# A routed low-rank residual layer: one subtraction per tile moved from GpSimd to VectorE, and another moved forward in VectorE's order

## The chip, the cores and the metric

The kernel runs on one core of one Trainium2 chip. The time is the device time of one execution in microseconds, and of several executions the median is taken. Beside it stands one profiled execution, whose trace is read here. Five engines work side by side, each with its own in-order queue: TensorE (PE in the profile; its weight loads are listed apart as PEld and overlap the matmuls), VectorE (DVE), ScalarE (ACT), GpSimd (POOL) and SyncE (SP), which here only issues transfers. They meet through semaphores.

## The reference

For each of 2048 tokens x (512 values), with one language id per sequence:

```
base   = x @ W.T                                        # 512 x 512
logits = x @ Wr.T + 5 * one_hot(language)               # 8 experts
topw, topi = top_k(logits, 2);  weights = softmax(topw)
gates  = sum over the two of one_hot(topi) * weights    # 8 gates
h      = einsum("btd,erd->bter", x, A)                  # 8 experts x rank 16
lora   = einsum("bter,bte,eor->bto", h, gates, B)
out    = x + base + 2 * lora
```

All of it is fp32, and the routing has to pick the right two experts.

## The kernel before

The tokens are cut into 16 tiles of 128. Each fp32 operand of a product is split in two: an upper part (`x_hi`, `w_hi`, `b_hi`, `ghT_hi`), which is the value rounded to the type that PE multiplies (fp32r), and a lower part (`x_lo` and so on), which is the value minus its upper part, rounded the same way. A product is then three: upper by upper, upper by lower, lower by upper. The contraction of 512 is cut into four chunks, so a block of products has 12 matmuls.

**PE.** For a tile t, "heads" is the block of 12 products that gives the upper half of the output columns (256), the 128 values of h and the 8 logits, together 392 columns, into `heads_ps`. "Base" is the block of 12 for the other 256 output columns, into `base_ps`. A step t (L575) is: heads of t, then the six lora products of tile t-3 (`lora`, L543: four with `ghT_hi` at L550, two with `ghT_lo` at L554, added on top of `heads_ps` and `base_ps` of tile t-3), then base of t. Before the heads of t come waits for `x_hi`, for `x_lo` and for `heads_ps` of tile t-4 to have been read (`heads_ready`, L565). Steps 3 and 4 are written out, steps 5 to 12 are a loop of two passes over four steps (L660), and the last three tiles are a sequence of their own.

**ScalarE** rounds `x_hi` (L271), makes `ghT_hi` from the turned gated values (L277), and takes the exponential for the softmax (L287). In its queue, iteration t is: `ghT_hi(t-3)`, `x_hi(t+1)`, exponential of t.

**GpSimd** makes `x_lo` (L232): one subtraction of 128x512 for each of the tiles 2 to 15, each as soon as the `x_hi` of that tile is there. The first two tiles go by chunks.

**VectorE** splits the weights at the start, and then does for each tile: `best_two` (L354: logits L358, the two largest with their places, the denominator), `gates` (L372, with `second` L375 and `gate` L380), `gated` (L388: `gh`, the 128 values of h times their gates), `in_blocks` (L351: 32x32 blocks of `gh` transposed), `ghT_lower` (L337: `ghT_lo`), `out_rest` (L401) and `out_base` (L407), which add x to the two halves of the output. The order by hand for an iteration t of 5 to 11 is: `ghT_lower(t-3)` (not in the first), `out_rest(t-3)`, `best_two(t)`, `gates(t)`, `gated(t)`, `out_base(t-3)`, `in_blocks(t)`. The last tiles have an order of their own (L476 to L510).

**SyncE** issues the loads of x and its transpose, and for tiles 1 to 13 a round trip that completes the transpose of `gh`: the blocks are stored to `gh_blocks` (L178, waits for `in_blocks(t)`), and when that has landed they are read back in turned order to `ghT` (L182); behind it on the same queue stands the store of tile t-3, which waits for `out_base(t-3)`.

`x_hi` and `x_lo` have four slots each, as have `heads_ps` and `base_ps`.

Of the kernel before, what the change touches and what calls it, by code (L numbers as in the profile page):

```python
# [4 lines left out]
FP32 = mybir.dt.float32  # L5
# [12 lines left out]
TILES = TOKENS // P  # L18
# [7 lines left out]
BATCH = 3  # L26
SQUARE = 32
PAIRS = 6
X_LOADS = {3: (6, 3), 5: (9, 3), 7: (12, 4)}
LANG_BIAS = 5.0  # L30
SCALING = 2.0
# [11 lines left out]
def cond_resid_program(nc: bass.Bass, first: bass.AP, xT: bass.AP, x: bass.AP,  # L43
# [11 lines left out]
    with ctx:  # L55
# [6 lines left out]
        def sem(name):  # L62
            return ctx.enter_context(nc.semaphore(name))
# [63 lines left out]

        x_hi_made = sem("x_hi_made")
        x_lo_made = sem("x_lo_made")
        heads_done = sem("heads_done")  # L130
        base_done = sem("base_done")
        logits_made = sem("logits_made")
# [89 lines left out]
        @block.gpsimd  # L222
        def _(pool):
            nc.gpsimd.memset(ident[:, :], 0.0).then_inc(ident_zeroed, 1)
            nc.gpsimd.iota(expert[:, :], pattern=[[1, E]], base=0, channel_multiplier=0).then_inc(expert_made, 1)
            pool.wait_ge(ident_zeroed, 1)
            nc.gpsimd.affine_select(out=ident[:, :], in_=ident[:, :], compare_op=ALU.not_equal, fill=1.0, base=0,
                                    pattern=[[-1, P]], channel_multiplier=1).then_inc(ident_made, 1)

            def x_lower(t, s):  # L230
                pool.wait_ge(x_hi_made, t - 1)
                nc.gpsimd.tensor_tensor(x_lo[:, s, :], xT_sb[:, t - len(FIRST), :], x_hi[:, s, :].bitcast(FP32),  # L232
                                        ALU.subtract).then_inc(x_lo_made, 1)

            def chunk_lower(k, tiles):
                nc.gpsimd.tensor_tensor(x_lo[:, tiles, chunks[k]], first_x[k][:, tiles, :],
                                        x_hi[:, tiles, chunks[k]].bitcast(FP32), ALU.subtract).then_inc(chunk_lo_made, 1)

            for k in range(KC):
                pool.wait_ge(chunk_hi_made, k + 1)  # L240
                if k == 1:
                    chunk_lower(k, slice(0, 1))
                    chunk_lower(k, slice(1, 2))
                else:
                    chunk_lower(k, slice(0, 2))
            pool.wait_ge(b_lo_made, 1)
            x_lower(2, 2)
            x_lower(3, 3)
            with pool.Fori(0, TILES // SLOTS - 1) as g:
                for j in range(SLOTS, 2 * SLOTS):  # L250
                    x_lower(SLOTS * g + j, j % SLOTS)

        @block.scalar
        def _(act):
# [77 lines left out]
        def _(dve):  # L332
            def ghT_lower(t):
                s = t % SLOTS
                if t in MOVED:
                    dve.wait_ge(ghT_hi_made, t + 1)
                    nc.vector.tensor_tensor(ghT_lo[s][:, :], ghT[s][:, :], ghT_hi[s][:, :].bitcast(FP32),  # L337
                                            ALU.subtract).then_inc(ghT_lo_made, 1)
                elif t < MOVED[0]:
                    dve.wait_ge(ghT_hi_made, t + 1)  # L340
                    nc.vector.tensor_tensor(ghT_lo[s][:, :], ghT_ps[t], ghT_hi[s][:, :].bitcast(FP32),
                                            ALU.subtract).then_inc(ghT_lo_made, 1)
                else:
                    dve.wait_ge(tail_hi_made, t - MOVED[-1])
                    nc.vector.tensor_tensor(ghT_lo[s][:, :], ghT_ps[t], ghT_hi[s][:, :].bitcast(FP32),
                                            ALU.subtract).then_inc(tail_lo_made, 1)

            def in_blocks(t, s):

# [4 lines left out]
            def best_two(t):  # L354
                s = t % SLOTS

                dve.wait_ge(heads_done, t + 1)
                nc.vector.tensor_tensor(logits[:, :], heads_ps[s][:, HEADS - E:HEADS], bias[:, :],  # L358
                                        ALU.add).then_inc(logits_made, 1)

                dve.wait_ge(bias_made, 1)
                dve.wait_ge(logits_made, t + 1)
                nc.vector.max(top[:, :], logits[:, :]).then_inc(top_made, 1)  # L363
                dve.wait_ge(bias_made, 1)
                dve.wait_ge(top_made, t + 1)
                nc.vector.max_index(top_at[:, :], top[:, :], logits[:, :]).then_inc(top_at_made, 1)  # L366
                dve.wait_ge(top_at_made, t + 1)
                nc.vector.tensor_copy(top_atf[:, :], top_at[:, 0:2]).then_inc(top_atf_made, 1)
                dve.wait_ge(e2_made, t + 1)
                nc.vector.tensor_scalar(den[:, :], e2[:, :], 1.0, 1.0 / SCALING, ALU.add, ALU.mult).then_inc(den_made, 1)  # L370
# [23 lines left out]
            def out_rest(t):  # L394
                s = t % SLOTS
                dve.wait_ge(lora_heads_done, t + 1)
                if t < 2 * BATCH:
                    dve.wait_ge(x_first[t // BATCH], 16)
                else:
                    dve.wait_ge(x_group, 16 * min(t // BATCH - 1, len(X_LOADS)))  # L400
                nc.vector.tensor_tensor(out_sb[:, t, BASE:O], heads_ps[s][:, 0:REST], x_sb[:, t, BASE:O],  # L401
                                        ALU.add).then_inc(heads_read, 1)

            def out_base(t):
                s = t % SLOTS
                dve.wait_ge(lora_base_done, t + 1)
                nc.vector.tensor_tensor(out_sb[:, t, 0:BASE], base_ps[s][:, 0:BASE], x_sb[:, t, 0:BASE],  # L407
                                        ALU.add).then_inc(out_made, 1)
# [56 lines left out]
            in_blocks(4, 0)  # L465
            t0, t1, t2 = range(TILES - 3, TILES)
            for t in range(LAG + 2, t0 - 1):
                if t > LAG + 2:
                    ghT_lower(t - LAG)
                out_rest(t - LAG)  # L470
                best_two(t)
                gates(t)
                gated(t)
                out_base(t - LAG)
                in_blocks(t, t % SLOTS)
            ghT_lower(t0 - 4)  # L476
            best_two(t0 - 1)
            out_rest(t0 - 4)
            gates(t0 - 1)
# [1 line left out]
            in_blocks(t0 - 1, (t0 - 1) % SLOTS)  # L481
            out_base(t0 - 4)
            ghT_lower(t0 - 3)
            best_two(t0)
            ghT_lower(t0 - 2)
            out_rest(t0 - 3)
# [2 lines left out]
            in_blocks(t0, t0 % SLOTS)  # L489
            out_base(t0 - 3)  # L490
            out_rest(t0 - 2)
            out_base(t0 - 2)
            ghT_lower(t0 - 1)
            best_two(t1)
# [18 lines left out]
        def _(pe):  # L513
# [50 lines left out]

            def heads_ready(t):  # L565
                pe.wait_ge(x_hi_made, t - 1)
                pe.wait_ge(x_lo_made, t - 1)
                if not (isinstance(t, int) and t < SLOTS):
                    pe.wait_ge(heads_read, t - SLOTS + 1)

# [86 lines left out]
            pe.wait_ge(b_lo_made, 1)  # L657
            step(3, 3 + SLOTS)
            step(4, 4)
            with pe.Fori(0, 2) as g:  # L660
                for j in range(5, 5 + SLOTS):
                    step(SLOTS * g + j, j)

            t0, t1, t2 = range(TILES - 3, TILES)
            s0, s1, s2 = t0 % SLOTS, t1 % SLOTS, t2 % SLOTS
# [48 lines left out]
```

## Time and profile before

| | us |
|---|---|
| median of 3 runs | 79.38 |
| the runs | 79.21, 79.38, 79.9 |
| the profiled execution, its own time | 79.19 |
| its span, first to last instruction | 77.4 |
| PE busy | 73.3 (95%) |
| VectorE busy | 57.0 (74%) |
| GpSimd busy | 22.5 (29%) |
| ScalarE busy | 21.4 (28%) |
| mean traffic with HBM | 205 GB/s |

The busy time of PE is the time in which at least one matmul is under way. In a timeline row the first number is the start in us from the span's start, the second the duration; an entry in brackets at its end is the idle time of the engine just before and who ended it. Rows do not carry tile numbers: the tile follows from the order of the queue. A line such as L554 is the line of the kernel printed above.

### The profile page before, as it was taken

Reading aid. Unit: us, or ns where it says so; the run is one execution under the profiler, and the core shown is the slowest. Engines: PE = TensorE matmul, PEld = TensorE weight load, DVE = VectorE, ACT = ScalarE, POOL = GpSimd, SP = SyncE. Lnnn points to the kernel's source line nnn. Section 1 sums busy time; section 2 is a strip of 40 time slices with the busy share of each in tenths; the row PEclk is TensorE's granted clock in tenths of the full one; section 3 lists DMA queues with packets and bytes.
Section 4 is the critical chain, followed back from the end, with each engine's and each line's share of the span. In section 5 each row is a group of like instructions: output and inputs, shape, how many; then the busy total and the mean of one; then the engine's idle time right before and its main releaser. Section 6 shows DMA issues by size and latency. Waiting matters only on the chain.

```text
span 77.4 us, 1531 instructions
## 1 busy us (share of the span) xinstructions
PE 73.3 (95%) x489; PEld 69.8 (90%) x489; DVE 57.0 (74%) x233; ACT 21.4 (28%) x56; POOL 22.5 (29%) x26
## 2 busy tenths in 40 slices
PE   5989999999999999799999999999999999999960
PEld 2259999999999999699999999999999999999950
DVE  0098486898698989786766949375889889888860
ACT  1570964024231305050143214050505051103100
POOL 4044539301450511505033600623154114000000
PEclk9999999999999999999999999999999999999999
DMA  1999999301374799889949799526872315166073
GB/s 15 306 395 350 415 416 432 124 8 34 66 200 110 123 354 273 277 222 320 278 161 258 246 304 367 148 104 203 237 236 46 129 36 168 34 215 227 7 271 136
DMA packets 14214, 15.96 MB, mean 206 GB/s; under 512 B 7680, under 2 KB 10368, under 8 KB 14080
## 3 DMA queue, kind: packets, MB, share of 16 engines
q1 hardware_dynamic: 13920, 15.35, 62.0%
q10 hardware_dynamic: 288, 0.53, 1.9%
q8 instruction: 3, 0.05, 0.2%
q14 instruction: 3, 0.02, 0.1%
HBM read 10.84 MB, written 5.05 MB: 205 GB/s over the span
## 4 chain that ended last, share of the span: by engine, by line
PE 80%; DVE 10%; DMA 4%; issue 2%; DVEq 0%
PE heads_ps L518 38%; PE base_ps L518 26%; PE base_ps L550 4%; PE heads_ps L550 4%; DMA first_sb<-in_first 4%; PE heads_ps L554 3%; PE heads_ps L593 2%; PE base_ps L554 2%; DVE gate L380 2%; DVE ghT_lo L337 2%; DVE gh L388 1%; DVE blocks L351 1%; DVE out_sb L407 1%; DVE top_at L366 1%; DVE second L375 1%
## 5 line engine op out<-in xcount | busy, mean ns | idle before, releaser
L232 POOL TENSOR_TENSOR x_lo<-xT_sb,x_hi 128x512 fp32r<-128x512 f32 x14 | 18.2, 1301 | 36.3 <-ACT x_hi L271 34.9
L518 PE MATMUL heads_ps<-w_hi,x_hi 128*128 128x392 f32 x63 | 21.8, 354 | 0.0
L518 PE MATMUL heads_ps<-w_lo,x_hi 128*128 128x392 f32 x63 | 20.9, 340 | 0.0
L518 PE MATMUL heads_ps<-w_hi,x_lo 128*128 128x392 f32 x63 | 20.5, 339 | 0.0
L518 PE MATMUL base_ps<-w_hi,x_lo 128*128 128x256 f32 x64 | 17.6, 281 | 0.0
L518 PE MATMUL base_ps<-w_hi,x_hi 128*128 128x256 f32 x64 | 17.5, 283 | 0.0
L518 PE MATMUL base_ps<-w_lo,x_hi 128*128 128x256 f32 x64 | 17.4, 280 | 0.0
L287 ACT ACTIVATE e<-top 128x1 f32<-128x1 f32 x16 | 4.7, 295 | 38.5 <-DVE top L363 38.5
L518 PEld LDWEIGHTS base_ps<-w_hi,x_hi 128*128 128x128 f32 x64 | 12.1, 190 | 0.4 <-issue 0.3
L518 PEld LDWEIGHTS heads_ps<-w_hi,x_hi 128*128 128x128 f32 x63 | 11.8, 190 | 0.5 <-issue 0.5
L518 PEld LDWEIGHTS base_ps<-w_lo,x_hi 128*128 128x128 f32 x64 | 12.1, 189 | 0.0
L518 PEld LDWEIGHTS base_ps<-w_hi,x_lo 128*128 128x128 f32 x64 | 11.9, 188 | 0.0
L518 PEld LDWEIGHTS heads_ps<-w_lo,x_hi 128*128 128x128 f32 x63 | 11.7, 188 | 0.0
L518 PEld LDWEIGHTS heads_ps<-w_hi,x_lo 128*128 128x128 f32 x63 | 11.7, 188 | 0.0
L401 DVE TENSOR_TENSOR out_sb<-heads_ps,x_sb 128x256 f32<-128x256 f32 x16 | 6.7, 418 | 5.4 <-PE heads_ps L554 5.4
L271 ACT ACTIVATE x_hi<-xT_sb 128x512 fp32r<-128x512 f32 x14 | 8.6, 617 | 1.1 <-DMA xT_sb<-in_xT 1.1
L380 DVE SCALAR_TENSOR_TENSOR gate<-expert,top_atf,second 128x8 f32<-128x8 int32 x16 | 7.4, 462 | 0.0
L388 DVE SCALAR_TENSOR_TENSOR gh<-heads_ps,rden,gate 128x128 f32<-128x128 f32 x16 | 5.6, 350 | 1.6
L407 DVE TENSOR_TENSOR out_sb<-base_ps,x_sb 128x256 f32<-128x256 f32 x16 | 6.6, 412 | 0.0
L411 DVE TENSOR_TENSOR w_lo<-first_sb,w_hi 128x392 fp32r<-128x392 f32 (+1 forms) x8 | 4.5, 596 | 1.6 <-ACT w_hi L259 1.5
L375 DVE TENSOR_SCALAR second<-expert,top_atf,e 128x8 f32<-128x8 int32 x16 | 5.5, 347 | 0.0
L351 DVE STREAM_TRANSPOSE blocks<-gh 128x128 f32<-128x128 f32 x13 | 5.2, 401 | 0.2
(46 smaller groups left out, 92.5 us busy)
## 6 DMA issues: line engine op xcount, KB each, us to landing
out<-out_sb SPq DMA_DIRECT2D x14, 256.0 KB, 2.5
x_sb<-in_x SPq DMA_DIRECT2D x4, 768.0 KB, 7.8
xT_sb<-in_xT SPq DMA_DIRECT2D x5, 512.0 KB, 4.6
x_sb<-in_x SPq DMA_DIRECT2D x1, 1024.0 KB, 6.1
first_sb<-in_first SPq DMA_DIRECT2D x2, 454.0 KB, 5.9
gh_blocks<-blocks SPq DMA_DIRECT2D x13, 64.0 KB, 1.5
ghT<-gh_blocks SPq DMA_DIRECT2D x13, 64.0 KB, 2.1
xT_sb<-in_xT SPq DMA_DIRECT2D x1, 768.0 KB, 8.0
```

The source lines that it names most:

```text
L232: nc.gpsimd.tensor_tensor(x_lo[:, s, :], xT_sb[:, t - len(FIRST), :], x_hi[:, s, :].bitcast(FP32), ALU.subtract).then_inc(x_lo_made, 1)
L271: nc.scalar.activation(x_hi[:, s, :], xT_sb[:, t - len(FIRST), :], ACT.Copy).then_inc(x_hi_made, 1)
L287: nc.scalar.activation(e2[:, :], top[:, 0:1], ACT.Exp, scale=-1.0, bias=top[:, 1:2]).then_inc(e2_made, 1)
L351: nc.vector.transpose(blocks[s][:, :].rearrange("p (j c) -> p j c", c=SQUARE), gh[s][:, :].rearrange("p (r j) -> p j r", r=SQUARE)).then_i ...
L375: nc.vector.tensor_scalar(second[:, :], expert[:, :], top_atf[:, 1:2], e2[:, :], ALU.is_equal, ALU.mult).then_inc(second_made, 1)
L380: nc.vector.scalar_tensor_tensor(gate[:, :], expert[:, :], top_atf[:, 0:1], second[:, :], ALU.is_equal, ALU.add).then_inc(gate_made, 1)
L388: nc.vector.scalar_tensor_tensor(gh[s][:, :].rearrange("p (e r) -> p e r", r=R), heads_ps[s][:, REST:REST + ER].rearrange("p (e r) -> p e ...
L401: nc.vector.tensor_tensor(out_sb[:, t, BASE:O], heads_ps[s][:, 0:REST], x_sb[:, t, BASE:O], ALU.add).then_inc(heads_read, 1)
L407: nc.vector.tensor_tensor(out_sb[:, t, 0:BASE], base_ps[s][:, 0:BASE], x_sb[:, t, 0:BASE], ALU.add).then_inc(out_made, 1)
L411: nc.vector.tensor_tensor(w_lo[:, k, cols], w_sb[:, k, cols], w_hi[:, k, cols].bitcast(FP32), ALU.subtract).then_inc(w_lo_made, 1)
L518: return nc.tensor.matmul(dst, xs[:, s, chunks[k]], ws[:, k, cols], start=(k == 0 and n == 0), stop=(k == KC - 1 and n == last_n))
L550: nc.tensor.matmul(dst, ghT_hi[s][:, :], bs[:, cols], start=False, stop=False, skip_group_check=True)
```

## The change

GpSimd keeps the subtractions of tiles 2 to 5 (`LOW_BY_POOL = 6`). Those of tiles 6 to 15 are made by VectorE with the same operands, and count on a semaphore of their own, `later_x_lo_made`, for which `heads_ready` waits from tile 6 on. On VectorE, `x_lower(t+1)` stands behind `out_rest(t-3)` and ahead of `best_two(t)`; in the last tiles it stands at three places written by hand. Further, `ghT_lower` of tile t-2 now stands directly behind `gated(t)`, ahead of `out_base(t-3)` and `in_blocks(t)`; before, the same instruction followed those two, at the head of iteration t+1. Since the number of the semaphore to wait for depends on the tile, PE's loop over steps 5 to 12 is written out.

```diff
--- before.py
+++ after.py
@@ -26,6 +26,7 @@
 BATCH = 3
 SQUARE = 32
 PAIRS = 6
+LOW_BY_POOL = 6
 X_LOADS = {3: (6, 3), 5: (9, 3), 7: (12, 4)}
 LANG_BIAS = 5.0
 SCALING = 2.0
@@ -127,6 +128,7 @@
 
         x_hi_made = sem("x_hi_made")
         x_lo_made = sem("x_lo_made")
+        later_x_lo_made = sem("later_x_lo_made")
         heads_done = sem("heads_done")
         base_done = sem("base_done")
         logits_made = sem("logits_made")
@@ -244,11 +246,8 @@
                 else:
                     chunk_lower(k, slice(0, 2))
             pool.wait_ge(b_lo_made, 1)
-            x_lower(2, 2)
-            x_lower(3, 3)
-            with pool.Fori(0, TILES // SLOTS - 1) as g:
-                for j in range(SLOTS, 2 * SLOTS):
-                    x_lower(SLOTS * g + j, j % SLOTS)
+            for t in range(len(FIRST), LOW_BY_POOL):
+                x_lower(t, t % SLOTS)
 
         @block.scalar
         def _(act):
@@ -344,6 +343,12 @@
                     dve.wait_ge(tail_hi_made, t - MOVED[-1])
                     nc.vector.tensor_tensor(ghT_lo[s][:, :], ghT_ps[t], ghT_hi[s][:, :].bitcast(FP32),
                                             ALU.subtract).then_inc(tail_lo_made, 1)
+
+            def x_lower(t):
+                s = t % SLOTS
+                dve.wait_ge(x_hi_made, t - 1)
+                nc.vector.tensor_tensor(x_lo[:, s, :], xT_sb[:, t - len(FIRST), :], x_hi[:, s, :].bitcast(FP32),
+                                        ALU.subtract).then_inc(later_x_lo_made, 1)
 
             def in_blocks(t, s):
 
@@ -465,15 +470,15 @@
             in_blocks(4, 0)
             t0, t1, t2 = range(TILES - 3, TILES)
             for t in range(LAG + 2, t0 - 1):
-                if t > LAG + 2:
-                    ghT_lower(t - LAG)
                 out_rest(t - LAG)
+                x_lower(t + 1)
                 best_two(t)
                 gates(t)
                 gated(t)
+                ghT_lower(t - LAG + 1)
                 out_base(t - LAG)
                 in_blocks(t, t % SLOTS)
-            ghT_lower(t0 - 4)
+            x_lower(t0)
             best_two(t0 - 1)
             out_rest(t0 - 4)
             gates(t0 - 1)
@@ -481,6 +486,7 @@
             in_blocks(t0 - 1, (t0 - 1) % SLOTS)
             out_base(t0 - 4)
             ghT_lower(t0 - 3)
+            x_lower(t1)
             best_two(t0)
             ghT_lower(t0 - 2)
             out_rest(t0 - 3)
@@ -489,6 +495,7 @@
             in_blocks(t0, t0 % SLOTS)
             out_base(t0 - 3)
             out_rest(t0 - 2)
+            x_lower(t2)
             out_base(t0 - 2)
             ghT_lower(t0 - 1)
             best_two(t1)
@@ -564,7 +571,10 @@
 
             def heads_ready(t):
                 pe.wait_ge(x_hi_made, t - 1)
-                pe.wait_ge(x_lo_made, t - 1)
+                if t < LOW_BY_POOL:
+                    pe.wait_ge(x_lo_made, t - 1)
+                else:
+                    pe.wait_ge(later_x_lo_made, t - LOW_BY_POOL + 1)
                 if not (isinstance(t, int) and t < SLOTS):
                     pe.wait_ge(heads_read, t - SLOTS + 1)
 
@@ -657,9 +667,8 @@
             pe.wait_ge(b_lo_made, 1)
             step(3, 3 + SLOTS)
             step(4, 4)
-            with pe.Fori(0, 2) as g:
-                for j in range(5, 5 + SLOTS):
-                    step(SLOTS * g + j, j)
+            for t in range(5, TILES - 3):
+                step(t, t)
 
             t0, t1, t2 = range(TILES - 3, TILES)
             s0, s1, s2 = t0 % SLOTS, t1 % SLOTS, t2 % SLOTS
```

## Rows read from the trace of the kernel before

**Rows 1.** Windows: us; PE, PEld, DVE, ACT, POOL busy (count); clock; DMA share; GB/s
```profile
10.00:15.00 5.00, 5.00 (x34) 5.00 (x33) 4.25 (x14) 1.76 (x4) 2.82 (x3) 1.00 0.84 350
30.00:35.00 5.00, 4.51 (x32) 4.31 (x31) 4.07 (x17) 1.59 (x5) 1.61 (x2) 1.00 0.81 237
65.00:70.00 5.00, 5.00 (x34) 4.96 (x33) 4.37 (x20) 0.49 (x2) 0.00 (x0) 1.00 0.39 125
```

**Rows 2.** Waits of PE's weight loads: waiter, releaser, total us, times, longest us
```profile
PEld base_ps L588 <- issue: 2.1, 6, 0.7
...
PEld heads_ps L554 <- DVE ghT_lo L337: 0.7, 1, 0.7
```

**Rows 3.** Timeline around step 6's hole: start us, duration us, engine, line
```profile
30.75 1.28 POOL L232 TENSOR_TENSOR x_lo<-xT_sb,x_hi 128x512 fp32r<-128x512 f32 x1 [3.36 <-ACT x_hi L271]
...
31.10 1.07 DVE L337 TENSOR_TENSOR ghT_lo<-ghT,ghT_hi 128x128 fp32r<-128x128 f32 x1
...
32.23 0.19 PEld L554 LDWEIGHTS heads_ps<-b_hi,ghT_lo 128*128 128x128 f32 x1 [0.69 <-DVE ghT_lo L337]
```

**Rows 4.** Timeline of PE: first heads product of steps 6, 7, 9
```profile
28.98 0.34 PE L518 MATMUL heads_ps<-w_hi,x_hi 128*128 128x392 f32 x1
...
33.98 0.34 PE L518 MATMUL heads_ps<-w_hi,x_hi 128*128 128x392 f32 x1
...
42.48 0.34 PE L518 MATMUL heads_ps<-w_hi,x_hi 128*128 128x392 f32 x1
```

**Rows 5.** Lines L337 and L380 (ns min/median/max), and one L380 of the timeline
```profile
L337 DVE TENSOR_TENSOR ghT_lo<-ghT,ghT_hi x13: 249/291/1073, 21.7 to 70.6; 128x128 fp32r<-128x128 f32 x13
...
L380 DVE SCALAR_TENSOR_TENSOR gate<-expert,top_atf,second x16: 225/227/1189, 14.3 to 71.3; 128x8 f32<-128x8 int32 x16
...
26.23 1.18 DVE L380 SCALAR_TENSOR_TENSOR gate<-expert,top_atf,second 128x8 f32<-128x8 int32 x1
```

**Rows 6.** Subtractions: groups by line (busy us, mean ns), and L411 by itself
```profile
L232 POOL TENSOR_TENSOR x_lo<-xT_sb,x_hi 128x512 fp32r<-128x512 f32 x14 | 18.2, 1301 | 36.3 <-ACT x_hi L271 34.9 <-DVE b_lo L438 1.5
...
L438 DVE TENSOR_TENSOR b_lo<-b_sb,b_hi 128x512 fp32r<-128x512 f32 x1 | 0.7, 692 | 0.0
...
L411 DVE TENSOR_TENSOR w_lo<-first_sb,w_hi x8: 410/493/1058, 4.4 to 10.6; 128x392 fp32r<-128x392 f32 x4, 128x256 fp32r<-128x256 f32 x4
```

**Rows 7.** Timeline of step 7: VectorE, and PE's first load of heads(8)
```profile
36.90 0.42 DVE L401 TENSOR_TENSOR out_sb<-heads_ps,x_sb 128x256 f32<-128x256 f32 x1 [0.78 <-PE heads_ps L554]
...
37.25 0.16 DVE L358 TENSOR_TENSOR logits<-heads_ps,bias 128x8 f32<-128x8 f32 x1
...
38.12 0.19 PEld L518 LDWEIGHTS heads_ps<-w_hi,x_hi 128*128 128x128 f32 x1
...
38.92 0.35 DVE L388 SCALAR_TENSOR_TENSOR gh<-heads_ps,rden,gate 128x128 f32<-128x128 f32 x1
...
39.52 0.39 DVE L351 STREAM_TRANSPOSE blocks<-gh 128x128 f32<-128x128 f32 x1
...
39.83 0.25 DVE L337 TENSOR_TENSOR ghT_lo<-ghT,ghT_hi 128x128 fp32r<-128x128 f32 x1
```

**Rows 8.** Timeline of step 10: `ghT_hi` of tile 7 and PE's loads that need it
```profile
47.61 0.31 ACT L277 ACTIVATE ghT_hi<-ghT 128x128 fp32r<-128x128 f32 x1 [1.11 <-DMA ghT<-gh_blocks]
...
48.67 0.19 PEld L550 LDWEIGHTS heads_ps<-b_hi,ghT_hi 128*128 128x128 f32 x1
...
49.21 0.19 PEld L554 LDWEIGHTS heads_ps<-b_hi,ghT_lo 128*128 128x128 f32 x1
```

**Rows 9.** Timeline of the tail: logits(12), gate(12), ghT_lo(12), the load behind it
```profile
57.54 0.17 DVE L358 TENSOR_TENSOR logits<-heads_ps,bias 128x8 f32<-128x8 f32 x1 [0.20 <-PE heads_ps L518]
...
59.14 1.17 DVE L380 SCALAR_TENSOR_TENSOR gate<-expert,top_atf,second 128x8 f32<-128x8 int32 x1
...
66.58 0.28 DVE L337 TENSOR_TENSOR ghT_lo<-ghT,ghT_hi 128x128 fp32r<-128x128 f32 x1
...
66.91 0.19 PEld L554 LDWEIGHTS heads_ps<-b_hi,ghT_lo 128*128 128x128 f32 x1
```

## The prediction

> **What bounds the kernel now.** I read the table of stretches first. PE is busy 5.00 of 5.00 us in eleven of the twelve 5 us stretches from 10 to 70 us, the first and the last of which are shown; the twelfth, 30 to 35 us, has 4.51. The granted clock is 1.00 in each, so no number here is a clock effect [rows 1]. So the kernel is bound by PE's own work, with one hole, and the question is what made it. The list of waits names it: the weight load of the lora product L554 waited once, 0.7 us, for `ghT_lo` of L337 [rows 2]. The timeline shows why. GpSimd's `x_lo` of tile 7 runs from 30.75 to 32.03. VectorE's `ghT_lo` of tile 3 starts inside it, at 31.10, and takes 1.07 us [rows 3]; the median of this line is 0.291 [rows 5]. It ends at 32.17 and the weight load starts at 32.23, so a waiting PE wakes in 0.06 us [rows 3]. It is the same clash elsewhere: `gate` took 1.18 us at 26.23, where its median is 0.227 [rows 5], and 1.17 us at 59.14 [rows 9]; those two cost PE nothing, as VectorE was ahead of it there.
>
> **The hole, worked out.** Heads of step 6 begin at 28.98, those of step 7 at 33.98: 5.00 us. From step 7 to step 9 it is 8.50, so 4.25 us for a step with no wait [rows 4]. The hole costs 0.75 us. PE waits for nobody else between 17 us and the end, so this is nearly all that a change away from PE's own work can win there.
>
> **Part 1: GpSimd's ten subtractions for tiles 6 to 15 go.** They took 1.30 us each [rows 6], off PE's path. With them go all clashes after 26 us: `gate` of tile 4 falls from 1.18 to 0.23, `ghT_lo` of tile 3 from 1.07 to 0.28. GpSimd keeps tiles 2 to 5, so the earlier clashes stay.
>
> **Part 2: VectorE makes them, directly behind `out_rest`.** No row shows this operation there, but `b_lo` (L438) has its shape and types (128x512 fp32 minus fp32 to fp32r, all in SBUF) and took 0.692 us on VectorE. Bounds: below, 0.41, the fastest w_lo (L411), half as wide; above, 1.06, the slowest of that line, 392 wide [rows 6]. I take 0.69, the row of the same shape. An instruction starts about 0.08 us before the one ahead ends (`out_rest` at 36.90 takes 0.42 and the next starts at 37.25 [rows 7]), so each adds 0.61 to the queue.
>
> The Trainium skill, "VectorE: DVE Perf Modes", section "The TRN2 errata", has a table that would make it (58 + 512)/0.96 = 594 ns, an estimate by that page; the row is 98 ns above, and the row decides. By the table the spare time worked out next would be 0.22 in place of 0.12 us.
>
> What it meets in a step, with step 7 as the pattern: `out_rest` starts at 36.90, as soon as L554 is done, the next instruction at 37.25. There `x_lower(8)` runs 37.25 to 37.94; with 0.06 to wake PE that is 38.00. PE's first weight load of heads(8) comes at 38.12 [rows 7]. So it is hidden behind the twelve base products with 0.12 us to spare, and shows from a duration of 0.81 us on. This is the tightest cover of the change, met in seven steps (x_lower of tiles 6 to 12). Its input is no issue: ScalarE makes x_hi a step ahead; the latest, of tile 11, follows `ghT_hi(7)`, done at 47.92 [rows 8], so even at 1 us is done by 48.95, and x_lower(11) would start at 37.25 - 0.75 + 3 x 4.25 = 49.25.
>
> The same page, section "The DRAIN you can't avoid", says that a next operation starts only when the pipe is empty. By that `x_lower` would start 0.07 later and the spare would be 0.05. The overlap in rows 7 speaks against it, and I keep 0.12.
>
> **Part 3: VectorE's total per step.** From `out_rest` at 36.90 to the end of `ghT_lo`, 39.83 + 0.25 = 40.08, it needs 3.18 us [rows 7]. With 0.61 that is 3.79 against PE's 4.25: 0.46 us of idle time stay, so VectorE does not become the bound. The first step of the new kind: `gate(4)` now ends at 26.46, gh and the transpose behind it (0.35 and 0.4) by 27.3. Heads(6) at 28.98 [rows 4] have their load 0.11 earlier, 28.87, and L554 is done 38.12 - 36.90 = 1.22 before that: `out_rest(2)` starts at 27.65, `x_lower(6)` ends at 28.69. The next instruction starts at 28.61, gh(5) 38.92 - 37.25 = 1.67 later [rows 7] at 30.28, and `ghT_lo(3)`, now directly behind it, at 30.55 to 30.83. PE wants it at 32.23 - 0.75 = 31.48 [rows 3]. The hole is closed with 0.6 us to spare.
>
> **Part 4: `ghT_lower` moved before `out_base` and `in_blocks`.** In its step gh stood 2.02 behind `out_rest`, the transpose 2.62 [rows 7]. With x_lower gh is at 2.63, `ghT_lo` at 2.90, `out_base` 3.10, the transpose 3.43: 0.81 later in its step, while PE is 0.75 earlier. On the clock the two cancel (tile 7: 39.52 before [rows 7], 36.15 + 3.43 = 39.58 after), its store leaves SP when it did, and so do the load behind it and the store of `out` behind that. The turned blocks land when they did, and PE asks for them 0.75 us sooner. The latest is tile 7: ScalarE waited 1.11 us for its DMA and made `ghT_hi` from 47.61 to 47.92. PE's L550 load stood at 48.67 and would stand at 47.92 [rows 8]: with waking, PE waits about 0.05 us. `ghT_lower(7)`, reached by VectorE at 36.15 + 2 x 4.25 + 2.90 = 47.55, waits until 47.95 and ends at 48.23; PE wants it at 49.21 - 0.75 = 48.46 [rows 8]. Queued behind it, out_base(6) and the transpose of tile 9 slip by 0.4 us, inside the idle 0.46; PE wants out_base's result a step later, and SP waits for the transpose. I take +0.05. Bounds: 0 (the blocks of tile 4 are ready 0.95 earlier, and what queues behind them on SP may go sooner), +0.5 where the slip of 0.4 reaches a transfer that PE needs.
>
> **Part 5: the tail.** `x_lower(13)` follows the transpose of tile 11 and ends near 57.6; heads(13), 33.98 + 6 x 4.25 = 59.48 [rows 4], want it near 58.6 with the hole gone. logits(12) start near 57.5, as before. From there to `ghT_lo(12)` it was 66.58 - 57.54 = 9.04 us [rows 9]; less two clashes of 0.93 (the one at 59.14, and tile 13's like it), with two x_lower of 0.61, it is 8.4, so 65.9 to 66.2 with its own 0.28. PE wants it at 66.91 - 0.75 = 66.16 [rows 9], as tightly as before, when it ended at 66.86 for a load at 66.91. I take 0, bound +0.1. The rest of the tail moves forward with PE, whose work is unchanged.
>
> **Part 6: PE's loop is written out.** Removed: two passes over four steps, with a branch and waits on a register's value. Steps 7 to 9 span the pass boundary (8 to 9) at 4.25 us a step [rows 4], as within a pass: nothing to win. Added: some 240 PE instructions of code, each once. The idle time put down to issue has 0.7 us as its longest piece, in the warm-up L588 [rows 2]; the straight-line steps 3 and 4 run inside the full stretches of rows 1. I take 0, upper bound 0.7.
>
> **Sum**: -0.75 + 0.05 + 0 + 0 = -0.70 us. The profiled execution took 79.19, so 78.49; the median of the runs shown is 79.38, 0.19 above it, so 78.68, 0.9% less. About 1% is what a measurement of this kernel can tell from no change.
>
> **Rivals.** (A) *x_lower misses its slot, slower.* Place: the start of heads of tiles 6 to 12, seven times. For: 0.12 us of cover, and a narrower w_lo reached 1.06. Against: GpSimd subtracted beside that one, and b_lo took 0.69. Each 0.1 us beyond 0.81 costs 0.7 in all: at 0.92 the gain is gone (79.4), at 1.04 it is 1.6 - 0.75 = 0.85 us slower (80.2). Chance 0.1. (B) *the hole moves to the turned blocks*: PE waits for `ghT_hi` of tile 7 and perhaps another, since DMA and not VectorE sets that time. For: a spare of -0.05. Against: SP may send earlier. Price 0.2 to 0.5: 78.9 to 79.15. Chance 0.22. (C) *the written-out code starves PE*, one hole of 0.3 to 0.7 us: 79.0 to 79.4, and the change does not do what the profile promises. Chance 0.1. Forecast: 0.58.
>
> **Chances.** The 1% bound lies at 78.59, 0.09 us below my point, and splits the forecast: 0.2 faster by over 1%. The rest of it (0.38), B (0.2), C (0.05) and A's near part (0.03) lie within 1%: 0.66. Slower: A's far part 0.07, and 0.07 for B and C several times over. The range runs from 78.4 (no wait for tile 7 and a slightly earlier tail) to 79.6, past A's break-even.
>
> **What would show it.** Right: no PE wait on L337; 5.00 in 30 to 35 us; `gate` and `ghT_lo` near 0.3 us at most after 26 us; x_lo on VectorE ten times at 0.69. Wrong: steps over 4.25 us with PE waiting for x_lo (A), L550 waiting for `ghT_hi` (B), issue holes in PE after 24 us (C).

## The result, and the profile after

The changed kernel is slower: median 80.72 us of 4 runs (80.03 to 81.78) against 79.47 us of 4 runs of the kernel before (79.21 to 79.9). The ratio is 1.0156, with a 95% interval of 1.0098 to 1.0215. Forecast were 78.68 us, a range of 78.4 to 79.6, and 0.14 for slower. Five more rounds beside other kernels gave 1.016 again (1.0099 to 1.0221). Single executions of one kernel scatter here by 1 to 4%, so a ratio is read with its interval, and where PE lost time is read from profiles. The profiled executions of `a4_unroll_only`, `b2_small_delay` and `d1_changed_quarters` were 1.8% or more above the fastest of their kernel; nothing is taken from them but the start of x_lo(4), the duration of gate(2) and the waits of PE in steps 3 and 4.

The waits of PE and its weight loads in the changed kernel (waiter, releaser, total us, times, longest), where before had the one of 0.7 us for `ghT_lo` [rows 2]:

```profile
PEld base_ps L598 <- issue: 2.1, 6, 0.7
...
PEld heads_ps L557 <- ACT ghT_hi L276: 0.9, 2, 0.6
PEld heads_ps L525 <- issue: 0.9, 3, 0.3
PEld heads_ps L561 <- DVE ghT_lo L336: 0.5, 1, 0.5
```

(L561 is the product that was L554, L557 was L550.) The table of stretches (columns as in [rows 1]): the hole at 30 to 35 us is gone, and two others are there, at 20 to 25 and at 45 to 50 us; a smaller one, at 60 to 65 us, has 4.92 of 5.00.

```profile
20.00:25.00 5.00, 4.62 (x31) 4.25 (x30) 4.33 (x16) 1.02 (x3) 1.29 (x1) 1.00 0.54 140
...
30.00:35.00 5.00, 5.00 (x36) 5.00 (x35) 4.12 (x21) 1.88 (x6) 0.00 (x0) 1.00 0.92 279
...
45.00:50.00 5.00, 4.70 (x34) 4.38 (x33) 3.29 (x15) 1.13 (x3) 0.00 (x0) 1.00 0.80 280
```

The first of them, in the timeline (start us, duration us, engine, line):

```profile
17.67 0.30 ACT L286 ACTIVATE e<-top 128x1 f32<-128x1 f32 x1 [0.96 <-DVE top L368]
...
18.54 1.33 DVE L385 SCALAR_TENSOR_TENSOR gate<-expert,top_atf,second 128x8 f32<-128x8 int32 x1
18.56 1.28 POOL L234 TENSOR_TENSOR x_lo<-xT_sb,x_hi 128x512 fp32r<-128x512 f32 x1 [4.89 <-ACT x_hi L270]
...
20.24 0.41 DVE L406 TENSOR_TENSOR out_sb<-heads_ps,x_sb 128x256 f32<-128x256 f32 x1
...
20.77 0.19 PEld L525 LDWEIGHTS heads_ps<-w_hi,x_hi 128*128 128x128 f32 x1 [0.29 <-issue]
```

Here `gate` of tile 2 takes 1.33 us where it needs 0.23, because GpSimd's x_lo(4) starts 0.02 us behind it. `out_rest(0)`, three instructions later, ends at 20.65 and not near 19.5; it frees the `heads_ps` slot that heads(4) need, and their first load comes 0.29 us late. The profile puts this down to issue; what it is, is `heads_read` (in the profile of `b1_pool_unrolled`, below, the same wait is named: 0.4 us for `out_sb`). The second clash follows from the first, as VectorE's order against GpSimd has shifted:

```profile
22.41 1.29 POOL L234 TENSOR_TENSOR x_lo<-xT_sb,x_hi 128x512 fp32r<-128x512 f32 x1 [2.56 <-ACT x_hi L270]
...
22.55 1.30 DVE L336 TENSOR_TENSOR ghT_lo<-ghT,ghT_hi 128x128 fp32r<-128x128 f32 x1
...
23.91 0.19 PEld L561 LDWEIGHTS heads_ps<-b_hi,ghT_lo 128*128 128x128 f32 x1 [0.46 <-DVE ghT_lo L336]
```

The same three instructions in the kernel before, where gate(2) took its usual time:

```profile
17.94 0.29 ACT L287 ACTIVATE e<-top 128x1 f32<-128x1 f32 x1 [1.26 <-DVE top L363]
...
18.82 0.23 DVE L380 SCALAR_TENSOR_TENSOR gate<-expert,top_atf,second 128x8 f32<-128x8 int32 x1
...
18.97 1.30 POOL L232 TENSOR_TENSOR x_lo<-xT_sb,x_hi 128x512 fp32r<-128x512 f32 x1 [4.69 <-ACT x_hi L271]
```

From the exponential of tile 2, which releases both chains, gate(2) stands at 0.88 before and 0.87 after. x_lo(4) stands at 1.03 before and at 0.89 after. That 0.14 us is the whole difference, and it comes from GpSimd's code (`b1_pool_unrolled`, below): before, tiles 4 to 15 were a loop whose waits compare with a register's value; after, tiles 2 to 5 are written out, with constants. Which of the two, the loop or the register, costs the 0.14 us is not shown. x_hi(4) was done 0.21 us ahead of x_lo(4) before (18.14 + 0.62 to 18.97) and 0.07 us after (17.87 + 0.62 to 18.56).

Step 10, where the turned blocks of tile 7 are late, answering to [rows 8]:

```profile
43.48 0.37 SPq L184 DMA_DIRECT2D ghT<-gh_blocks  x1
...
49.12 0.31 ACT L276 ACTIVATE ghT_hi<-ghT 128x128 fp32r<-128x128 f32 x1 [1.84 <-DMA ghT<-gh_blocks]
...
49.48 0.19 PEld L557 LDWEIGHTS heads_ps<-b_hi,ghT_hi 128*128 128x128 f32 x1 [0.62 <-ACT ghT_hi L276]
```

And a plain step, answering to [rows 7]; here everything came as forecast:

```profile
37.08 0.42 DVE L406 TENSOR_TENSOR out_sb<-heads_ps,x_sb 128x256 f32<-128x256 f32 x1 [0.44 <-PE heads_ps L561]
37.42 0.68 DVE L350 TENSOR_TENSOR x_lo<-xT_sb,x_hi 128x512 fp32r<-128x512 f32 x1
38.02 0.16 DVE L363 TENSOR_TENSOR logits<-heads_ps,bias 128x8 f32<-128x8 f32 x1
...
38.29 0.19 PEld L525 LDWEIGHTS heads_ps<-w_hi,x_hi 128*128 128x128 f32 x1
```

`x_lower(8)` ends at 38.10 for a load at 38.29, `out_rest` waits 0.44 us each step (forecast: 0.46 of idle time), and the step is 4.25 us.

### The profile page after: what moved, and what is told of

Its sections match the earlier page's. It is cut to its first block, busy times and chain, and to the rows that moved or that the text cites. A ratio compares the mean times of both kernels' runs of the same rounds, so it can differ in the third digit from the quotient of the medians.

```text
span 78.8 us, 1483 instructions
## 1 busy us (share of the span) xinstructions
PE 74.6 (95%) x489; PEld 70.3 (89%) x489; DVE 59.6 (76%) x243; ACT 21.9 (28%) x56; POOL 9.4 (12%) x16
## 4 chain that ended last, share of the span: by engine, by line
PE 65%; DVE 18%; DMA 10%; issue 3%; ACT 0%; DVEq 0%
PE heads_ps L525 27%; PE base_ps L525 20%; DMA ghT<-gh_blocks 7%; PE heads_ps L557 4%; PE base_ps L598 4%; PE base_ps L557 4%; DMA gh_blocks<-blocks 3%; PE heads_ps L561 2%; DVE gate L385 2%; PE heads_ps L603 2%; DVE top_atf L373 2%; PE base_ps L561 2%; DVE ghT_lo L336 2%; DVE top_at L371 2%; DVE out_sb L412 1%
## 5 line engine op out<-in xcount | busy, mean ns | idle before, releaser
L350 DVE TENSOR_TENSOR x_lo<-xT_sb,x_hi 128x512 fp32r<-128x512 f32 x10 | 6.8, 680 | 0.0
L234 POOL TENSOR_TENSOR x_lo<-xT_sb,x_hi 128x512 fp32r<-128x512 f32 x4 | 5.1, 1291 | 8.9 <-ACT x_hi L270 7.5
L336 DVE TENSOR_TENSOR ghT_lo<-ghT,ghT_hi 128x128 fp32r<-128x128 f32 x13 | 4.7, 363 | 1.6 <-ACT ghT_hi L276 1.6
L276 ACT ACTIVATE ghT_hi<-ghT 128x128 fp32r<-128x128 f32 x13 | 3.9, 303 | 5.7 <-DMA ghT<-gh_blocks 5.7
```

Of the source, the lines that this page charges most:

```text
L276: nc.scalar.activation(ghT_hi[s][:, :], ghT[s][:, :], ACT.Copy).then_inc(ghT_hi_made, 1)
L350: nc.vector.tensor_tensor(x_lo[:, s, :], xT_sb[:, t - len(FIRST), :], x_hi[:, s, :].bitcast(FP32), ALU.subtract).then_inc(later_x_lo_made, 1)
```

## The experiments

The first theory, from this profile: the loss is one of places and moments (T: early clashes, late turned blocks, the order of the tail), not of VectorE's load (rival V). Others: only the early clashes (E), the move of `ghT_lower` (M), PE's longer code (C).

To compare profiles whose start differs by some tenths of a us with the landing of the first loads, I take from each timeline the time from the first heads product of step 3 to the transpose of tile 14 on PE (16.12 to 69.41 in before, 53.29 us). Less its hole of 0.75 that is 52.54, which `c3_quarters`, with no wait in it, measured too. What lies above is waiting; the part up to the heads of step 5 (8.62 us without waits) stands apart. Where a cell is empty, the profile is not used for it.

| kernel | ratio to before (95%) | PE waits, steps 3 and 4, us | PE waits behind, us |
|---|---|---|---|
| before | 1 | 0 | 0.75 |
| changed, first profile | 1.0156 (1.0098 to 1.0215) | 0.90 | 1.29 |
| a1, changed again | 1.016 (1.0099 to 1.0221) | 1.24 | 1.57 |
| a2, move only | 0.9941 (0.9897 to 0.9985) | 0.10 | 0.14 |
| a3, x_lower on VectorE, no move | 1.0116 (1.0068 to 1.0165) | 1.23 | 0.41 |
| a4, PE's loop written out | 0.9995 (0.996 to 1.0029) | 0 | |
| b1, GpSimd's loop written out | 1.0171 (1.0091 to 1.0251) | 1.21 | 0.96 |
| b2, changed, x_lo(4) 0.06 us later | 0.9954 (0.9914 to 0.9994) | 0 | |
| b3, changed, tail order | 1.0047 (1.0006 to 1.0089) | 1.29 | 0 |
| b4, changed, turned blocks first | 1.1787 (1.1721 to 1.1853) | | |
| c1, b2 and b3 together | 0.9859 (0.9769 to 0.995) | 0 | 0.49 |
| c2, no GpSimd behind tile 3 | 0.9896 (0.983 to 0.9961) | 0.13 | 0.05 |
| c3, before, GpSimd in quarters | 0.9874 (0.9816 to 0.9931) | 0 | 0 |
| d1, changed, GpSimd in quarters | 0.9974 (0.9934 to 1.0013) | 0 | |

**The parts by themselves.** `a1_changed_again` is the changed kernel.

> The changed kernel itself, a second profile of it beside its parts. Its first profile had six waits of PE behind step 3: 0.28 and 0.52 us where GpSimd's x_lo of tiles 4 and 5 met VectorE's gate(2) and ghT_lo(1), 0.55 us for ghT_hi(7) out of the DMA, and 0.23, 0.14 and 0.25 us in the last four tiles. Theory T (late transfers and order, not VectorE's load): the waits in the tail and for ghT_hi of tile 7 come again (0.9 us together, within 0.4), the two early ones may fall elsewhere, since they hang on where a GpSimd subtraction starts; time 1.0 to 1.6% above before. Rival V (VectorE is overloaded in each step): steps 6 to 10 are longer than 4.25 us. Rival E (the early clashes are the whole loss): with them gone, the time is at or below that of before.

The ratio came again. gate(2) took 1.33 us and ghT_lo(1) 1.31, as in the first profile; in step 10 the weight load waited 1.30 us for ghT_hi(7), and the step was 1.23 us longer; heads(13) were 0.22 us late. Steps 5 to 9 took 4.24 to 4.25 us each, and step 10, but for that wait, no more. So V falls; the early clashes did not fall elsewhere, they came in the same place.

`a2_move_only`:

```diff
@@ before.py, VectorE, iterations 5 to 11
-                if t > LAG + 2:
-                    ghT_lower(t - LAG)
                 out_rest(t - LAG)
                 best_two(t)
                 gates(t)
                 gated(t)
+                ghT_lower(t - LAG + 1)
                 out_base(t - LAG)
                 in_blocks(t, t % SLOTS)
-            ghT_lower(t0 - 4)
```

> The kernel before with ghT_lower moved behind gated, and nothing else; GpSimd still makes all x_lo. ghT_lo(3) then starts at 30.45, ahead of GpSimd's subtraction at 30.75, so the hole of 0.75 us goes by the place alone; what then overlaps the subtraction are out_base (one input in PSUM) and the transpose, which took 0.41 us beside GpSimd before too. The transposes are 0.2 us later in their step, not 0.8. Theory T: 0 to 0.3 us of new waits for turned blocks, so 0.5 to 0.9% below before. Rival V says the same of this one (no work is added). Rival M (the move is what hurts, because it delays the transposes): above before.

The move alone is a gain, 0.6%. Its step 6:

```profile
30.51 0.28 DVE L337 TENSOR_TENSOR ghT_lo<-ghT,ghT_hi 128x128 fp32r<-128x128 f32 x1
...
30.70 1.30 POOL L232 TENSOR_TENSOR x_lo<-xT_sb,x_hi 128x512 fp32r<-128x512 f32 x1 [3.26 <-ACT x_hi L271]
...
31.05 0.40 DVE L351 STREAM_TRANSPOSE blocks<-gh 128x128 f32<-128x128 f32 x1
```

`ghT_lo(3)` is through before GpSimd starts, the transpose behind it takes 0.40 us beside GpSimd, and PE does not wait in this step. M falls.

`a3_vector_only` is the changed kernel with those lines put back.

> The changed kernel with ghT_lower back in its old place at the head of the next iteration; x_lower stays on VectorE. No clash can come after tile 5, so the hole at step 6 is gone all the same. The transposes are 0.6 us later in their step instead of 0.8, and out_rest(9) still stands behind x_lower(13) and best_two(12). Theory T: within 0.4% of the changed kernel. Rival M: it is at least 0.7% faster than the changed kernel.

1.0116, 0.4% below the changed kernel, with intervals that overlap: as T had it, and not the 0.7% of M. Its early clashes are those of the changed kernel (gate(2) 1.33 us, x_lo(4) 0.02 us behind it). `a4_unroll_only` has before's loop of PE written out, and nothing else.

> The kernel before with PE's loop over steps 5 to 12 written out, nothing else. All theories but one: within 0.3% of before, with the same hole of 0.75 us at step 6. Rival C (longer code makes PE wait for its instructions, or its fetches disturb the transfers): 0.5% or more above before.

0.9995. C falls.

What all kernels with a slow gate(2) share, and those without it lack, is GpSimd's written-out code. That gave theory S: the start of x_lo(4), 0.14 us earlier, makes the clash. `b1_pool_unrolled` is the kernel before with GpSimd's loop written out:

```diff
-            with pool.Fori(0, TILES // SLOTS - 1) as g:
-                for j in range(SLOTS, 2 * SLOTS):
-                    x_lower(SLOTS * g + j, j % SLOTS)
+            for t in range(SLOTS, TILES):
+                x_lower(t, t % SLOTS)
```

> The kernel before with GpSimd's loop over tiles 4 to 15 written out, nothing else. In the profiles of before, x_lo(4) starts 1.03 us behind the exponential of tile 2, 0.15 us behind the start of gate(2), which takes its usual 0.23 us. In all three profiles with the written-out code it starts 0.89 us behind the exponential, within 0.02 us of gate(2), and gate(2) takes 1.33 us; ghT_lo(1) then meets x_lo(5). Theory S (a start 0.14 us earlier makes the early clash): this kernel shows gate(2) at 1.33 us and PE waits of about 0.6 at step 4 heads and 0.5 at its L554, 0.8 to 1.1 us in all, less what the hole at step 6 may lose by the new timing: 0.3 to 1.2% above before. Rival L (VectorE's new work is the whole cause): no change, within 0.3%.

```profile
17.84 0.29 ACT L286 ACTIVATE e<-top 128x1 f32<-128x1 f32 x1 [1.28 <-DVE top L362]
...
18.72 1.32 DVE L379 SCALAR_TENSOR_TENSOR gate<-expert,top_atf,second 128x8 f32<-128x8 int32 x1
18.74 1.29 POOL L232 TENSOR_TENSOR x_lo<-xT_sb,x_hi 128x512 fp32r<-128x512 f32 x1 [4.56 <-ACT x_hi L270]
```

This edit, in which no instruction of a tile is added, moved or given to another engine, costs 1.7%, somewhat more than the 1.2% expected at most, and as much as the whole change. Rival L falls. `b2_small_delay` goes the other way, on the changed kernel:

```diff
                 pool.wait_ge(x_hi_made, t - 1)
+                if t == 4:
+                    nc.gpsimd.memset(spare[:, :], 0.0)
                 nc.gpsimd.tensor_tensor(x_lo[:, s, :], xT_sb[:, t - len(FIRST), :], x_hi[:, s, :].bitcast(FP32),
```

> The changed kernel with one small GpSimd memset (128x32, into a tile nobody reads) between the wait for x_hi(4) and x_lo(4), so that x_lo(4) starts about 0.1 us later. Theory S: gate(2) takes 0.23 us, and both early waits of PE (0.8 to 1.1 us together) are gone; the time falls by 0.8 to 1.4% against the changed kernel's 1.016, to 1.002 to 1.008 of before. Rival L: no change, 1.016. If 0.1 us is too little, gate(2) is as slow as before, and nothing is told.

0.9954: a memset of no use takes 2.0% off the changed kernel, and it is now faster than before, if by less than 1%. That is 1.6 us, more than the 0.8 to 1.4% expected and more than the 0.90 to 1.24 us of early waits; what else it brought is not shown. In its profile gate(2) takes 0.23 us, and PE waits for nothing in steps 3 and 4. The rows, from `c1_delay_and_tail`, which has the same memset:

```profile
17.77 0.29 ACT L289 ACTIVATE e<-top 128x1 f32<-128x1 f32 x1 [1.27 <-DVE top L371]
...
18.64 0.12 POOL L236 MEMSET spare<- 128x32 f32 x1 [4.54 <-ACT x_hi L273]
...
18.65 0.23 DVE L388 SCALAR_TENSOR_TENSOR gate<-expert,top_atf,second 128x8 f32<-128x8 int32 x1
...
18.72 1.31 POOL L237 TENSOR_TENSOR x_lo<-xT_sb,x_hi 128x512 fp32r<-128x512 f32 x1
```

The subtraction starts 0.07 us behind `gate` instead of 0.02, and gate takes 0.23 us. Between these two offsets lies 1.1 us of VectorE's time.

**The other waits.** `b3_tail_order` is the changed kernel with `out_rest(t0 - 4)` put ahead of `best_two(t0 - 1)`. In the changed kernel the order was:

```profile
58.35 0.65 DVE L350 TENSOR_TENSOR x_lo<-xT_sb,x_hi 128x512 fp32r<-128x512 f32 x1
...
58.92 0.16 DVE L363 TENSOR_TENSOR logits<-heads_ps,bias 128x8 f32<-128x8 f32 x1
...
59.87 0.41 DVE L406 TENSOR_TENSOR out_sb<-heads_ps,x_sb 128x256 f32<-128x256 f32 x1
...
60.40 0.19 PEld L525 LDWEIGHTS heads_ps<-w_hi,x_hi 128*128 128x128 f32 x1 [0.25 <-issue]
```

> The changed kernel with out_rest(9) ahead of best_two(12) in the tail. Both profiles of the changed kernel have heads(13) 0.22 us late, behind out_rest(9), which frees its heads_ps slot. Expected: base(12) to heads(13) takes 1.42 us and not 1.64; the time within 0.4% of the changed kernel's, 0.2 us below it at best, less than this measurement can tell; the profile decides. If heads(13) is late all the same, the wait is another one.

In its profile base(12) to heads(13) takes 1.41 us, and nothing behind step 4 waits. So the wait of 0.25 us was `out_rest(9)`. (The list of `a1_changed_again` puts the same wait down to `x_hi`; the one that ended there was x_hi(14), which heads(13) do not need.) The time fell by 1.1%, 0.9 us, more than the 0.2 us of the edit. Its profile had also no wait in step 10 and none in steps 13 to 15, where the changed kernel's first profile lost 0.55 and 0.51 beside the one for heads(13); the edit cannot reach step 10, so at least there the profile was a lucky one. What else the edit brings is not shown.

`b4_turn_first` swaps two issues on SyncE's queue of the changed kernel:

```diff
                 blocks_out(t)
+                ghT_in(t)
                 if t % 2 == 0 and PAIRS + t - 2 < TILES:
                 ...
-                ghT_in(t)
```

> The changed kernel with the order on SyncE's queue changed for tiles 1 to 13: the load of the turned blocks is issued ahead of the big load of x or its transpose, not behind it. Theory T (the 1 MB load of x in front of ghT(7) is what makes PE wait 0.55 and 1.14 us at L557 in step 10): ghT(7) lands 2 to 3 us after its issue and not 5.6, and PE waits for no ghT_hi; 0.5 to 1.3% below the changed kernel. Danger: the big loads then leave up to 2 us later, so x_hi or out_rest may wait for them; if PE waits for x_hi instead, the order before was a compromise of its own.

1.1787. The danger named there was the result, far beyond its size: `ghT_in` waits for the store of the blocks to land, and with it every big load behind it. The waits of the engines in its profile:

```profile
ACT x_hi L270 <- DMA xT_sb<-in_xT: 13.7, 6, 3.3
ACT ghT_hi L276 <- DMA ghT<-gh_blocks: 11.3, 8, 3.0
```

The time says nothing for or against the 1 MB load as the cause of the wait in step 10, but the profile speaks for it. ghT(7), issued ahead of the load, was in use 2.10 us later, as theory T had it:

```profile
52.12 0.37 SPq L184 DMA_DIRECT2D ghT<-gh_blocks  x1
...
54.22 0.31 ACT L276 ACTIVATE ghT_hi<-ghT 128x128 fp32r<-128x128 f32 x1 [0.90 <-DMA ghT<-gh_blocks]
```

In the other kernels, where the load is issued first, it took from the issue of ghT(7) to ghT_hi(7) 4.95 us in before, 5.64 in the changed kernel's first profile and 6.43 in its second, 4.65 in a2, 4.60 in a3, 4.51 in b1, 4.19 in b3, 5.77 in c1, 4.20 in c2 and 4.89 in c3. The load in front thus seems to account for 2 us and more; since the issues of `b4_turn_first` came late and its other transfers stood otherwise too, it is not shown to do so by itself. The time also scatters by 2.2 us between kernels that issue ghT(7) under like conditions, and by 0.8 us between two profiles of one kernel. Where it is long, PE, now earlier, waits. What makes it scatter stays open.

**Versions.** `c1_delay_and_tail` has both mends. `c2_all_on_vector` gives VectorE tiles 4 and 5 too:

```diff
-LOW_BY_POOL = 6
+LOW_BY_POOL = 4
             out_rest(0)
+            x_lower(4)
...
             out_rest(1)
+            x_lower(5)
```

> The changed kernel with both mends: the small memset ahead of x_lo(4), and out_rest(9) ahead of best_two(12). Theory S: no clash before tile 5's with a cost for PE, heads(13) on time; what is left is a wait for turned blocks in some executions. 0.2 us below the kernel with the memset alone (ratio 0.9954), so 0.992 to 0.996 of before. A profile with no wait of PE behind 16 us would have a span of 77.4 - 0.75 = 76.65 us, if the loads at the start land as in the first profile of before.

> The changed kernel with x_lo of tiles 4 and 5 on VectorE too (behind out_rest(0) and out_rest(1)), and out_rest(9) ahead of best_two(12). GpSimd then makes nothing behind tile 3, so no clash is possible behind 14 us whatever the start times. x_lo(4) would end near 19.9 and PE wants it at 20.4; x_lo(5) near 24.4 for 24.6. Theory S: 0.990 to 0.996 of before, with less spread than the other kernels. Rival V (VectorE is too full in the first steps): PE waits for x_lo(4) or (5), 0.2 to 0.5 us, and the time is that of before or above.

0.9859 and 0.9896, both faster than before by more than their intervals, if by less than 2%, like each other within them, and a little below what was expected. In c1's profile the only wait left behind step 3 is one of 0.6 us in step 10, for ghT_hi(7). There x_lo(5) still holds `second` of tile 3 (1.33 us), and PE does not wait for it: a clash costs time only where PE soon needs what stands behind it. In c2's no `gate`, `second` or `ghT_lo` behind 14 us takes over 0.3 us, and no step is more than 0.06 us longer for an x_lo: V falls. Its executions still scattered (78.52 to 80.61), so less spread is not shown.

`c3_quarters` asks how long a clash holds VectorE, in the kernel before:

```diff
-                nc.gpsimd.tensor_tensor(x_lo[:, s, :], xT_sb[:, t - len(FIRST), :], x_hi[:, s, :].bitcast(FP32),
-                                        ALU.subtract).then_inc(x_lo_made, 1)
+                for k in range(KC):
+                    last = nc.gpsimd.tensor_tensor(x_lo[:, s, chunks[k]], xT_sb[:, t - len(FIRST), chunks[k]],
+                                                   x_hi[:, s, chunks[k]].bitcast(FP32), ALU.subtract)
+                last.then_inc(x_lo_made, 1)
```

> The kernel before with each of GpSimd's subtractions from tile 2 on in four instructions of 128x128 instead of one of 128x512 (loop kept). If GpSimd holds VectorE off for one whole instruction, a clash costs VectorE at most a quarter (0.3 to 0.45 us) and the hole at step 6 shrinks from 0.75 to under 0.2 us: 0.3 to 0.8% below before. If it is held for as long as GpSimd is busy at all, the clashes stay at 1.1 to 1.3 us or grow with the longer sum (four times 0.5), and x_lo(4), 0.6 us later than now, makes PE wait at step 4.

0.9874, more than expected. GpSimd needs more (the four together 1.72 us for 1.30), and the longest `gate` and `ghT_lo` are (ns min/median/max):

```profile
L382 DVE SCALAR_TENSOR_TENSOR gate<-expert,top_atf,second x16: 225/228/377, 13.2 to 70.2; 128x8 f32<-128x8 int32 x16
...
L339 DVE TENSOR_TENSOR ghT_lo<-ghT,ghT_hi x13: 250/285/526, 21.1 to 69.5; 128x128 fp32r<-128x128 f32 x13
```

They were 1189 and 1073 in before [rows 5]. VectorE is held for one GpSimd instruction, not for as long as GpSimd is busy. Without moving any work, this kernel has no PE wait in the stretch of the table. `d1_changed_quarters` puts the same four lines into the changed kernel, where only tiles 2 to 5 use them.

> The changed kernel with GpSimd's four whole-tile subtractions (tiles 2 to 5) in quarters of 128x128, nothing else: x_lo(4) starts as early as in the changed kernel (0.89 us behind the exponential), but a clash can hold VectorE only for one quarter. Theory S with the holding time of one instruction: gate(2) takes 0.3 to 0.6 us and not 1.33, out_rest(0) and ghT_lo(1) are not late, the early waits of PE are under 0.2 us together, and the time is 0.993 to 0.999 of before, as with the small memset (0.9954). If an early start costs something else than the clash, it stays near 1.016. x_lo(4) takes 4 x 0.45 = 1.8 us in place of 1.3, ends near 20.3 on the clock of before and PE wants it at 20.4: at most 0.1 to 0.3 us of a new wait.

0.9974, level with before; x_lo(4) started 0.02 us behind gate(2), as in the changed kernel, and gate(2) took 0.50 us instead of 1.33. In its profile PE waits for nothing in steps 3 and 4. So neither the early start nor the move of the work costs what the change cost; the length of the clash does. E holds as it was put: with the early clash gone or short, the time is at (d1) or below (b2, c1) that of before. What the waits behind step 4 take, they take from the gain that was forecast.

## Why the prediction was wrong, point by point

**What bounds the kernel, and the hole**: right. PE's own work, and one hole of 0.75 us made by GpSimd beside `ghT_lo(3)`. It is gone in every kernel where `ghT_lo(3)` is free of the clash: the changed kernel, a2, a3, b3, c1, c2, c3.

**Part 1, the failing step**: "GpSimd keeps tiles 2 to 5, so the earlier clashes stay." The clashes of before were taken as tied to the tiles. They are tied to which instructions overlap, and that can turn on a few hundredths of a us; the change touched one: GpSimd's loop went with its ten tiles, so x_lo(4) came 0.14 us earlier and met gate(2), which in before it had missed. The term was put at nothing and measures 0.90 and 1.24 us of PE waits in steps 3 and 4 in two profiles. That alone is larger than the whole gain. `b1_pool_unrolled` shows that this edit by itself costs 1.7%, `b2_small_delay` that undoing it by 0.06 us gives 2.0% back. The diff shows the loop's removal in plain sight; part 6 weighed the same edit on PE and none of it on GpSimd.

**Part 2**: right. x_lo on VectorE took 0.680 us (0.69 taken), started 0.34 behind `out_rest`, and had 0.19 us of cover in the step shown (forecast 0.12). PE waits for it in no profile of the changed kernel. Rival A falls. The next instruction started 0.08 us before the end (38.02 against 38.10), as rows 7 had it. The Trainium skill's table for it ("VectorE: DVE Perf Modes", "The TRN2 errata", 594 ns) is 86 ns low here. The same section of the Trainium skill says that this row of the table is too low for a single instruction, and its formula for an fp32 `tensor_tensor`, (N + 151)/0.96, would have given 691 ns, 11 above the trace. The section "The DRAIN you can't avoid" of the same page of the Trainium skill was read by half in the prediction: it goes on that a next instruction which is not held starts earlier, and with that the trace agrees.

**Part 3**: right: 0.44 us of idle time per step for 0.46, ghT_lo(3) from 31.47 to 31.75 for a load at 32.40, 0.65 us to spare (forecast 0.6), no hole.

**Part 4**: the mechanism is right and the size wrong. PE did wait for ghT_hi(7) in step 10, as forecast, but 0.55 and 1.2 us, not 0.05. The landing was taken from one profile as if it were fixed; from issue to use it took 4.2 to 6.4 us in the ten profiles listed above, 5.64 and 6.43 in the two of the changed kernel. The bound of +0.5 was too narrow, since it knew only what VectorE could add. This is rival B, at a higher price than it was given (0.2 to 0.5).

**Part 5**: wrong. Heads(13) need, besides x_lo(13), the slot that `out_rest(9)` frees, and that instruction stands behind `x_lower(13)` and `best_two(12)`. By the prediction's own numbers logits(12) stay at 57.5, so `out_rest(9)`, 0.95 later, would end at 58.9 for a load at 58.6. That is a late 0.3 us; it measured 0.23 and 0.22. The list of what heads wait for has three entries, and only one was followed through the tail. ghT_lo(12) was late too in the first profile (0.5 us with ghT_hi(12), whose blocks came through a SyncE queue that was behind), and on time in the second.

**Part 6**: right for PE (0.9995), so rival C falls as it was put. Its kin on GpSimd was the cause.

**The sum**, for the first profile: -0.75 for the hole, +0.90 early, +0.55 in step 10, +0.23 for heads(13), +0.51 in steps 13 to 15, together +1.44; the span went from 77.4 to 78.8.

The device time rose by more, from 79.19 to 80.98, since a second term was put at nothing. The time outside the span, before the first or behind the last instruction, is 1.76 to 1.89 us in every execution of before and 2.13 to 2.28 in every one of the changed kernel: 0.35 us more. It is there in a3, b2, b3, b4, c1 and d1 too (2.10 to 2.28), not in a2, a4, b1 and c3 (1.76 to 1.90), and little of it in c2 (1.86 to 1.95). So neither a written-out loop by itself nor `ghT_lower` brings it; what does stays open. With the early clash taken away (b2), the ratio 0.9954 is that of a gain of 0.4 us, where 0.7 was forecast. Of the executions counted for it, the spans alone were 0.8 us shorter than those of before (medians 76.7 and 77.5), so the gain inside the span came, and 0.35 us of it was lost outside.

## What to carry to other kernels

When GpSimd and VectorE both work from SBUF, write down for each GpSimd instruction which VectorE instructions start while it runs or within 0.1 us ahead of it, on every tile, before and after an edit (held here were `gate`, `second`, `top_atf` and `ghT_lo`; `gh`, `out_rest`, `out_base` and the transpose were not); an edit that changes only how a loop is written moves these meetings, and one can cost more than the work that the edit was about. Cutting long GpSimd instructions into short ones bounds the price of every meeting at once. Here it did by itself (0.9874) what moving the work did only together with its mends (0.9859 and 0.9896; without them 1.016). When an engine is made earlier, follow all of its waits at each place, the freeing of slots too, and take a transfer's landing from several profiles, not from one. Compare the spans as well as the times: a difference outside the span shows in no row of a trace.

## What the runs showed of the hardware that I had not expected

- A VectorE instruction that has started can still lose. In the profiles used here GpSimd's 128x512 subtraction started 0.01 to 0.02 us behind a `gate` or a `second` eight times, and that instruction took 1.32 to 1.33 us each time (0.23 and 0.29 are usual). A start 0.05 to 0.08 us behind left `gate` (c1), `ghT_lo` (before) and `second` (b1) alone, but once, in b1, it held `second` for 1.42 us. A start 0.09 us or more behind held none:

```profile
27.00 1.42 DVE L374 TENSOR_SCALAR second<-expert,top_atf,e 128x8 f32<-128x8 int32 x1
...
27.08 1.32 POOL L232 TENSOR_TENSOR x_lo<-xT_sb,x_hi 128x512 fp32r<-128x512 f32 x1 [3.20 <-ACT x_hi L270]
```

- An instruction held by GpSimd is held until that one GpSimd instruction ends: for nearly 1.3 us with 128x512 where both start together, for what is left of it where VectorE comes later (`ghT_lo` 1.07 us in [rows 3]). With 128x128 the longest held instruction took 0.53 us, of which 0.29 is its own time.
- GpSimd's instruction started 0.07 to 0.09 us after its input was done in written-out code, and 0.17 to 0.21 us after it in a loop with waits on a register's value (12 tiles each, b1 and before).
- On the one DMA queue, putting the issue of a small transfer, which must wait for another to land, ahead of the large loads cost 14 us of 80 (b4).
